# A conditioned feed-forward kernel: the first block's gathered weights by row gathers and register-addressed DMAs in place of a round trip through DRAM

## The reference

```python
w = weights[conditions]                       # (128, 32, 32) from a table of 200 x 32 x 32
h0 = einsum('bct,bcd->bdt', x, w)             # x (128, 32, 256)
logits = h0 @ gate_w                          # gate_w (256, 8), the two largest are summed: scale
h = square(relu(h0 @ up_w))                   # up_w (256, 1024)
y = h @ down_w + scale * (h0 @ expert_weight) # down_w (1024, 256), expert_weight (256, 256)
out = x + (y - mean(y)) * rsqrt(var(y) + eps) * gamma + beta
```

## Time and profile before

| | |
|---|---|
| median of 3 runs | 238.65 us (238.57 to 238.71) |
| the profiled execution: its own time | 238.47 us |
| its span (first to last instruction) | 236.5 us |
| mean granted TensorE clock over the span | 0.985 of full speed |
| PE busy (matmuls) | 225.8 us, 96% of the span |
| DVE, ACT, POOL busy | 147.2, 107.2, 132.3 us |

### The profile page before, as it was taken

How to read it: one execution, slowest core, us unless ns; L and a number is a source line. 1 busy time by engine, 2 the same in 40 slices (tenths; PEclk the granted TensorE clock), 3 DMA queues, 4 the chain that set the end, 5 groups by cost and what they waited for, 6 DMA issues and landing times.

```text
span 236.5 us, 3575 instructions
## 1 busy us (share of the span) xinstructions
PE 225.8 (96%) x1250; PEld 193.3 (82%) x1250; DVE 147.2 (62%) x376; ACT 107.2 (45%) x184; POOL 132.3 (56%) x120
## 2 busy tenths in 40 slices
PE   7489999999999999999999999999999999999991
PEld 3178887888888888888888888888888988888991
DVE  1254696656667666566666666567666566666785
ACT  2247984554455444544444444544443544444200
POOL 4404877465644675365645675455754665566522
PEclk9959999999999999999999999999999999999999
DMA  5679991000110002000020002000020002000021
GB/s 189 199 231 229 204 346 48 4 1 0 48 43 0 1 0 91 1 0 0 13 79 0 3 0 89 1 3 0 1 89 3 0 0 89 4 0 0 35 79 67
DMA packets 15713, 12.95 MB, mean 55 GB/s; under 512 B 5168, under 2 KB 14896, under 8 KB 15696
## 3 DMA queue, kind: packets, MB, share of 16 engines
q1 hardware_dynamic: 15520, 12.14, 17.2%
q0 software_dynamic: 176, 0.59, 0.8%
HBM read 7.94 MB, written 4.78 MB: 54 GB/s over the span
## 4 chain that ended last, share of the span: by engine, by line
PE 86%; DMA 4%; DVE 3%; POOL 2%; issue 2%; ACT 1%; SPq 1%; POOLq 0%; DVEq 0%
PE up_ps L230 35%; PE down_ps L268 24%; PE down_ps L270 12%; PE hid_ps L217 5%; PE moe_ps L286 3%; PE moe_ps L284 3%; PE moe_ps L285 3%; DMA moe<-in_L_cond_weights_dram,cond_col 1%; POOL sq_lo L471 1%; DMA w_first_by_batch<-moe 1%; DVE down_hl L429 1%; DMA cond_col<-in_itok_B_dram 1%; DMA wd<-w_first_by_batch 1%; PE moe_ps L217 1%; POOL x_sb L480 1%
## 5 line engine op out<-in xcount | busy, mean ns | idle before, releaser
L471 POOL TENSOR_TENSOR sq_lo<-square,sq_hi 128x512 fp32r<-128x512 f32 x64 | 83.7, 1308 | 71.1 <-DVE square L369 70.8
L268 PE MATMUL down_ps<-down_hl,sq_hi 128*128 128x512 f32 x248 | 88.8, 393 | 0.3 <-POOL sq_lo L471 0.3
L270 PE MATMUL down_ps<-down_hl,sq_lo 128*128 128x256 f32 x248 | 69.6, 280 | 0.0
L369 DVE SCALAR_TENSOR_TENSOR square<-up_ps,relu 128x512 f32<-128x512 f32 x64 | 44.0, 687 | 38.3 <-ACT relu L323 38.3
L268 PEld LDWEIGHTS down_ps<-down_hl,sq_hi 128*128 128x128 f32 x248 | 46.5, 188 | 11.3 <-issue 0.7
L323 ACT ACTIVATE relu<-up_ps 128x512 f32<-128x512 f32 x64 | 38.2, 597 | 35.0 <-PE up_ps L230 34.7
L230 PE MATMUL up_ps<-hid_hi,up_hi 128*128 128x512 f32 x128 | 52.5, 410 | 0.0
L230 PE MATMUL up_ps<-hid_hi,up_lo 128*128 128x512 f32 x128 | 50.6, 395 | 0.0
L270 PEld LDWEIGHTS down_ps<-down_hl,sq_lo 128*128 128x128 f32 x248 | 46.7, 188 | 2.3
L325 ACT ACTIVATE sq_hi<-relu 128x512 fp32r<-128x512 f32 x64 | 40.5, 633 | 2.0
L230 PE MATMUL up_ps<-hid_lo,up_hi 128*128 128x512 f32 x128 | 40.0, 394 | 0.0
(11 more groups left out here) (44 smaller groups left out, 207.2 us busy)
## 6 DMA issues: line engine op xcount, KB each, us to landing
x_sb<-in_x_dram SPq DMA_DIRECT2D x8, 512.0 KB, 6.4
out_dram<-result SPq DMA_DIRECT2D x7, 512.0 KB, 2.9
result<-in_L_ffn_up_w_dram SPq DMA_DIRECT2D x2, 512.0 KB, 4.6
result<-in_L_ffn_down_w_dram SPq DMA_DIRECT2D x1, 1024.0 KB, 5.7
w_by_batch<-moe SPq DMA_DIRECT2D x1, 512.0 KB, 3.7
out_dram<-result SPq DMA_DIRECT2D x4, 128.0 KB, 1.7
wd<-w_by_batch SPq DMA_DIRECT2D x4, 96.0 KB, 5.9
eg_raw<-L_ffn_expert_weight_dram SPq DMA_DIRECT2D x1, 256.0 KB, 2.5
```

Source lines behind the costliest of these rows:

```text
L268: pe.matmul(dst[:, :], a_hi, down_hl[:, c, :, :].rearrange("p s t -> p (s t)"), start=(c == 0), stop=False)
L270: mm = pe.matmul(dst[:, T:2 * T], a_lo, down_hl[:, c, 0, :], start=False, stop=(c == CH - 1))
L369: dve.scalar_tensor_tensor(square[:, c % 2, :], up_ps[c % UPB][:, :], 0.0, relu[:, c % 2, :], ALU.max, ALU.mult).then_inc(square_done, 1)
L471: pool.tensor_tensor(sq_lo[:, j % 2, c, :], square[:, c % 2, :], sq_hi[:, j % 2, c, :].bitcast(f32), ALU.subtract).then_inc(sq_lo_done, 1)
```

## The change

- SP loads the first 16 conditions into one partition (`cond_row`), and then x of block 0. The full column `cond_col` is loaded later, behind the expert weights and the second half of up_w.
- ACT issues two DMAs at the start: `cond_span` (each partition p gets five conditions from number p // 32 on, so that the condition of its batch row in group 0 and in group 1 stand at two fixed places) and the first half of up_w. It then takes its table load with a small activation on `minus_half`.
- **Groups 0 and 1**: POOL fills `partition` with the partition's number (iota), DVE makes the row numbers `rows = 32 * condition + channel` from it, POOL gathers 128 rows of 128 bytes for each group into `w_pair` (channel to a partition already), and DVE copies four 32x32 pieces of each into `wd`.
- **Groups 2 and 3**: SP (group 2) and ACT (group 3) load four conditions each into registers and issue four DMAs each from the table straight into `wd`.
- `wd` of the later groups is zeroed on POOL behind the two row gathers; the gather of all 128 rows comes after that, and waits for `cond_col`. The write to `all_dram` and the reads of it follow on SP.
- `down_w` goes into the last eight groups of `x_sb`, so it needs no wait and is issued ahead of x of block 1. The x of the last two blocks waits for `down_lo_ready`. The four splits of down move to (0, 5), (0, 6), (0, 7), (1, 0).
- On PE the eight conditioning products of block 0 come in the order in which weights arrive, the first two up chunks are interleaved (`up_rounded`, `up_rest`), `WARM` is 20. On ACT and DVE `hidden(0, k)` stands ahead of the expert split, and `split_up(1)` behind the first chunk.

```diff
-WARM = 26
+WARM = 20
+SPLIT_DOWN_AT = [(0, 5), (0, 6), (0, 7), (1, 0)]
+PAIR = 2
+SPAN = Q * (PAIR - 1) + 1
...
-        down_raw = result_flat.rearrange("p (c t) -> p c t", c=CH)
+        down_raw = x_sb[:, GROUPS - CH:GROUPS, :]
...
+        def conditions(engine, g):
+            _, values = nc.values_load_multi_w_load_instructions(
+                cond_row[0:1, Q * g:Q * g + Q], [engine],
...
+        def weights_of(row):
+            return cond_w[bass.ds(row, 1), :, :].rearrange("s c d -> (s c) d")
...
         def _(sp):
-            sp.dma_start(cond_col[:, :], cond.rearrange("(b o) -> b o", o=1)).then_inc(cond_landed, 16)
+            sp.dma_start(cond_row[:, :], cond.rearrange("(o b) -> o b", o=1)[:, 0:TILES * Q]) \
+                .then_inc(cond_row_landed, 16)
             sp.dma_start(x_sb[:, groups(0), :], x_rows[:, groups(0), :]).then_inc(x_landed[0], 16)
-            sp.dma_start(up_raw[:, :, up_cols(0)], up_rows[:, :, up_cols(0)]).then_inc(up_landed[0], 16)
-
-            sp.wait_ge(first_gathered, 16)
-            sp.dma_start(first_dram, w_first).then_inc(first_written, 16)
-            sp.dma_start(up_raw[:, :, up_cols(1)], up_rows[:, :, up_cols(1)]).then_inc(up_landed[1], 16)
+            sp.wait_ge(cond_row_landed, 16)
+            values = conditions(mybir.EngineType.SP, PAIR)
             sp.wait_ge(wd_zeroed[0], 1)
-            sp.wait_ge(first_written, 16)
             for q in range(Q):
-                sp.dma_start(wd[C * q:C * q + C, groups(0), D * q:D * q + D], first_by_q[q]) \
-                    .then_inc(wd_landed[0], 16)
+                sp.dma_start(wd[C * q:C * q + C, PAIR, D * q:D * q + D], weights_of(values[q])) \
+                    .then_inc(wd_first_landed[PAIR], 16)
+
+            sp.wait_ge(pair_gathered[PAIR - 1], 16)
...
+            def conditioning_first():
+                pe.wait_ge(x_landed[0], 16)
+                pe.wait_ge(spread_done, Q)
+                condition(0, 0, 0)
+                condition(0, 1, 0)
+                pe.wait_ge(wd_first_landed[2], 16 * Q)
+                condition(0, 0, 2)
+                condition(0, 1, 2)
+                pe.wait_ge(wd_first_landed[3], 16 * Q)
+                condition(0, 0, 3)
+                pe.wait_ge(spread_done, 2 * Q)
+                condition(0, 0, 1).then_inc(hid_done, 1)
+                condition(0, 1, 3)
+                condition(0, 1, 1).then_inc(hid_done, 1)
...
+            act.dma_start(cond_span[:, :], bass.AP(tensor=cond.tensor, offset=0, ap=[[1, Q], [0, C], [1, SPAN]])) \
+                .then_inc(cond_pair_landed, 16)
+            act.dma_start(up_raw[:, :, up_cols(0)], up_rows[:, :, up_cols(0)]).then_inc(up_landed[0], 16)
...
+            dve.scalar_tensor_tensor(rows[:, :], cond_span[:, 0:SPAN:Q], float(C), chan[:, :].to_broadcast([P, PAIR]),
+                                     ALU.mult, ALU.add).then_inc(rows_ready, 1)
+            dve.wait_ge(wd_zeroed[0], 1)
+            for g in range(PAIR):
+                dve.wait_ge(pair_gathered[g], 16)
+                for q in range(Q):
+                    part = slice(C * q, C * q + C)
+                    dve.tensor_copy(wd[part, g, D * q:D * q + D], w_pair[part, g, :]).then_inc(spread_done, 1)
...
             pool.memset(minus_half[:, :], -0.5).then_inc(consts_ready, 1)
+            pool.iota(partition[:, :], pattern=[[0, 1]], base=0, channel_multiplier=1).then_inc(partition_ready, 1)
+            pool.wait_ge(rows_ready, 1)
+            for g in range(PAIR):
+                pool.indirect_dma_start(
+                    out=w_pair[:, g, :], out_offset=None, in_=table_rows,
+                    in_offset=bass.IndirectOffsetOnAxis(ap=rows[:, g:g + 1], axis=0)).then_inc(pair_gathered[g], 16)
+            pool.memset(wd[:, TILES:GROUPS, :], 0.0).then_inc(wd_zeroed[1], 1)
             pool.wait_ge(cond_landed, 16)
...
```

More of the change, by code:

```diff
@@ L60, in adaln_ffn @@
         cond_col = sb("cond_col", [P, 1], i32)
+        cond_row = sb("cond_row", [1, TILES * Q], i32)
+        cond_span = sb("cond_span", [P, SPAN], i32)
+        partition = sb("partition", [P, 1], i32)
+        chan = sb("chan", [P, 1], i32)
+        rows = sb("rows", [P, PAIR], i32)
+        w_pair = sb("w_pair", [P, PAIR, D])
+        table_loaded = sb("table_loaded", [P, 1])
         warm = sb("warm", [P, 512], bf16)
@@ L152, in last_tile @@
             return j == BLOCKS - 1 and t == TILES - 1
+        def conditions(engine, g):
+            _, values = nc.values_load_multi_w_load_instructions(
+                cond_row[0:1, Q * g:Q * g + Q], [engine],
+                skip_runtime_bounds_check_because="a condition is an index into the table by the kernel's contract")
+            return values
+        def weights_of(row):
+            return cond_w[bass.ds(row, 1), :, :].rearrange("s c d -> (s c) d")
         block = ctx.enter_context(nc.Block())
@@ L226, in up, with up_rest @@
                 wait(pe, square_done, CH * j + c - UPB + 1)
-                dst, par = up_ps[c % UPB][:, :], j % 2
-                def product(w, k, h, n):
-                    return pe.matmul(dst, w[:, k, P * c:P * c + P], h[:, par, k, :], start=(n == 0),
-                                     stop=(n == 3 * K - 1))
-                product(up_hi, 0, hid_hi, 0)
+                up_product(j, c, up_hi, 0, hid_hi, 0)
                 if j == 0 and c % (CH // UP_PARTS) == 0:
                     pe.wait_ge(up_lo_ready, c // (CH // UP_PARTS) + 1)
-                product(up_lo, 0, hid_hi, 1)
+                up_product(j, c, up_lo, 0, hid_hi, 1)
                 if c == 0:
                     pe.wait_ge(hid_hi_done, K * j + 2)
-                product(up_hi, 1, hid_hi, 2)
-                product(up_lo, 1, hid_hi, 3)
+                up_product(j, c, up_hi, 1, hid_hi, 2)
+                up_product(j, c, up_lo, 1, hid_hi, 3)
+            def up_rest(j, c):
                 if c == 0:
                     pe.wait_ge(hid_lo_done, K * j + 1)
-                product(up_hi, 0, hid_lo, 4)
+                up_product(j, c, up_hi, 0, hid_lo, 4)
                 if c == 0:
                     pe.wait_ge(hid_lo_done, K * j + 2)
-                product(up_hi, 1, hid_lo, 5).then_inc(up_done, 1)
+                up_product(j, c, up_hi, 1, hid_lo, 5).then_inc(up_done, 1)
+            def up(j, c):
+                if j == 0 and c == 0:
+                    up_rounded(j, 0)
+                    up_rounded(j, 1)
+                    up_rest(j, 0)
+                elif j == 0 and c == 1:
+                    up_rest(j, 1)
+                else:
+                    up_rounded(j, c)
+                    up_rest(j, c)
             def down(j, t, half):
@@ L439, in _ @@
                 .then_inc(eg_lo_ready, 1)
-            hidden(0, 0)
-            hidden(0, 1)
             for j in range(BLOCKS + 1):
@@ L460, in _ @@
                             finish(j - 1, c // 2 - 1)
-                    if j == 0 and c >= CH - DOWN_PARTS:
-                        split_down(c - (CH - DOWN_PARTS))
+                    if j == 0 and c == 1:
+                        split_up(1)
+                    if (j, c) in SPLIT_DOWN_AT:
+                        split_down(SPLIT_DOWN_AT.index((j, c)))
             finish(BLOCKS - 1, TILES - 1)
```

82 lines of the change are left out of this document (49 added, 33 removed).

## The result

| | before | changed |
|---|---|---|
| median | 238.61 us (238.10 to 238.71) | 245.56 us (244.89 to 246.40) |
| profiled execution, its span | 238.47, 236.5 us | 244.89, 242.7 us |

The ratio is 1.0297 (95% interval 1.0260 to 1.0334): 3% slower, where I had forecast no change (238.8) and a range that ended at 240.8.

The account below looks back on a forecast made before the run. PE was taken as the bound, so only its idle and half-clock time could be won. Start -1.46, gap -0.31 and clock +1.9 sum to +0.1 us: 238.8 us, no change, own range 238.0 to 239.6, with rivals 235.9 to 240.8.

Parts of the forecast that it names:

- Step 1: Front: cond_span, issued on ACT at about 0.73, lands between 2.75 and 4.05, taken as 3.4.
- Step 2: Front: row numbers at 3.85, gathers at 3.85 and 5.2; groups 0 and 1 land at 6.85 and 8.2.
- Step 3: Front: DVE's eight copies of 32x32 take 0.15 us each; the last four end at 8.9.
- Step 4: Front: groups 2 and 3 through registers land at 6.5 and about 7, hidden behind group 1.
- Step 5: PE: first weights at 7.5 at full clock, conditioning done at 9.7, ready for conditioning(1, 0) at 19.2 instead of 25.46.
- Block 1's chain, 24.0: Block 1's weights, through cond_col, gather, write and reads, let PE start conditioning(1, 0) at 24.0 (22.3 to 26).
- Clock, 1.9: Behind PE's 4.8 us idle before conditioning(1, 0), half clock costs between 0 and 2.6 us, taken as 1.9.
- The 0.31 gap goes, the moved split costs nothing: Block 1: PE's 0.31 us gap for sq_lo goes; the later last down split costs nothing, up to 0.6 without cover.
- From 25.46 the kernel is a fixed length of PE work: From conditioning(1, 0) on: fixed PE work plus a tail, so the change is worth that start's move, idle and clock aside.
- the second, POOL's configuration change: Rival: configuration change ahead of the iota, or other causes, delay second gather past 8.7; slower, 240.4 at 1.5 us; chance 0.21.
- The clock holds, or the chain is shorter: Rival: no clock drop in PE's idle time, 236.9, or block 1's chain 1 us shorter, 235.9; chance 0.29.
- not late: Rival: block 1's weights are not late, conditioning(1, 0) starts 6.3 us earlier, 232.5; chance 0.05.

Follow-up runs that it names:

- h2: Changed kernel with cond_span read by one DMA of outer count 128, eight conditions broadcast to all partitions: 243.72 us, ratio 1.0226.
- e4: Changed kernel with POOL's memset of wd's later groups moved behind the gather of all rows: 245.85 us.
- e5: Changed kernel with POOL's memset of wd's later groups moved right behind the iota: 245.84 us.
- e8: e7 with cond_span loaded by four DMAs of 32 partitions, as in e6: 238.66 us, ratio 1.0040.
- g2: e8 with x of block 1 issued ahead of down_w: 238.03 us, ratio 1.0000.
- g3: g2 with the four down splits back at chunks 4 to 7 of block 0: 237.16 us, ratio 0.9968.
- e1: Kernel before the change plus one unused tile of 480 bytes per partition ahead of warm: 239.61 us, ratio 1.0062.
- e2: Changed kernel with its seven new small tiles allocated last, behind result: 245.26 us.
- e6: Changed kernel with cond_span loaded by four DMAs of 32 partitions instead of one with outer count 4: 245.37 us.
- g1: Changed kernel with down_w and x of block 1 behind the write to DRAM, beta and gamma behind block 1's reads, cond_col left late: 247.47 us, ratio 1.0388.
- e7: Changed kernel with the edits of e3 and g1 together, POOL's memset behind the iota and small tiles allocated last: 238.47 us, ratio 1.0016.
- e3: Changed kernel with the load of cond_col moved ahead of x of block 0 on SP: 243.45 us, ratio 1.0228.

## Why the prediction was wrong

The mechanism was the one that I named: block 1's weights are late next, PE stops at `conditioning(1, 0)`, the clock dips there. The step that failed is the size of block 1's chain: it put the start at 24.0, and it was 28.59. One cost I had not looked for at all. Against the +0.1 of my sum, the start is 4.59 us later, the gap ahead of `down` 0.59 instead of nothing, the clock 0.34 cheaper and the addresses cost 1.05; with 0.18 unplaced that makes 6.1, and the span is 242.7 where the sum gives 236.6.

- **Step 1, `cond_span` at 3.4.** 5.36, above my upper bound of 4.05. I had named the cause, an outer count of four, and priced it by the packet time of a full queue, 0.65 us; h2 puts it at 1.94 (4.62 against 2.68). Worth 1.7 us of the total (h2).
- **Step 2, group 1 landing at 8.2.** SP goes on at 10.04, 1.84 later. The second gather went out at 7.37 instead of 5.2, 2.17 later, nearly all of it `cond_span`; it then took 2.7 us instead of 3.0.
- **Step 3, copies of 0.15.** Right for seven of eight (0.17); the first took 1.52. I read POOL's gathers ahead of the memset, but never asked what the memset, which now ran *with* the copies, does to them. Shown by e4 and e5; worth nothing in total, since block 1 binds.
- **Step 4, register path hidden.** Held: PE waited for DVE's copies, never for the register-addressed DMAs. The two register loads took 0.49 and 0.50 us, less than the 0.6 that I had cited as the least.
- **Step 5, PE ready at 19.2.** 25.98. The first conditioning ends at 15.77 instead of 9.7: 4.0 of this is that the copies end at 12.88 instead of 8.9 (steps 1 to 3), of the other 2.1, 1.7 is the clock at 0.53 over 3.56 us (3.56 x 0.47), which I had at full speed because I expected the weights by 7.5, and the other 0.4 I put down to the held first copy, which left PE nothing to do until then. From 15.77 to 25.98 are 0.7 us more than I had, and two waits show in them, 0.33 for the expert scaling and 0.39 for `up_lo`. It changed little by itself: e5 had PE ready 2.8 us earlier, and it only waited longer.
- **Block 1's chain, 24.0.** Start 28.59, +4.59: `cond_col` issued 1.8 late (steps 1 and 2), 4.4 instead of 2.7 to landing (+1.7), the gather 6.5 instead of 4.3 (+2.2), the write 2.7 instead of 3.7 (-1.0), the reads -0.1. For the gather I had written "up to 1 later since down_w and x move beside it" and then not put it in the sum. **This step decided the sign**; its upper bound of 26 left room for 2 us, and three links slipped by 5.7 together.
- **Clock, 1.9.** 1.56. Right in size, though behind a wait of 2.61 us and not the 4.8 that I argued from; that it came out so near is in part luck.
- **The 0.31 gap goes, the moved split costs nothing.** 0.59 instead of 0.31. e8 and g2, with the last split behind chunk 0 of block 1, show 0.6 and 0.55, g3 with it one chunk earlier has none: this was the 0.6, the bound that I gave for the split without its cover.
- **"From 25.46 the kernel is a fixed length of PE work."** False by 1.05 us: the new tiles change addresses, and PE runs slower on them (e1, e2). No row of before could show it, but the diff did: tiles allocated ahead of others are part of a change.

The rivals: the iota started at 0.86 and took 0.13 us, so the second, POOL's configuration change, had the right sign by a mechanism that did not occur, which is luck; what its last clause held, other causes that move the second gather past 8.7, did. "The clock holds, or the chain is shorter" and "not late" fell.

The part of the change that was to bring a gain can bring a small one: in g3, with the transfers ordered anew, block 1 starts 0.58 us earlier and the clock of the profiled execution stays full, for 0.3%, with an interval that nearly reaches no change.

## What to carry to other kernels

When a change shortens one chain, price the chain that is next with every transfer that now moves beside it, and put a slip of each link in the upper bound together, not one at a time. A transfer's place in the queue has no price of its own: here early conditions won 2.1 us and late bulk lost 1.9, and both together, with the memset out of their way, some 6. Allocate new small tiles behind the large ones, and compare the pace of an undisturbed block first, since it tells an address effect from a wait.

## What the runs showed of the hardware

- **Addresses change the pace of matmuls.** 480 bytes more ahead of `hid_hi` and the tiles behind it moved `up_ps<-hid_hi,up_lo` from 392 to 396 ns in the mean of the later blocks and the first `down` product from 392 to 394, the same in the changed kernel and in e1, and back in e2: 0.15 us in a block of 26.93. 480 is no multiple of 64, so the shift changes the remainder by 32. Whether this remainder is what matters, or another, was not tried.
- **A DVE copy stands still beside a POOL memset.** In h2 the memset stands at the same place in POOL's order and starts 1.42 us earlier than in the changed kernel, as all of the front does:

```profile
6.90 3.10 POOL L581 MEMSET wd<- 128x3584 f32 x1
```

  It ends at 10.00, and the copy from 8.40 ends at 10.03; in the changed kernel 11.42 and 11.45. In e6 the copy began at 8.69, took 2.75 us and ended at 11.44, the memset at 11.41. The copy isn't slowed but held to the memset's end. The Trainium skill (SBUF — State Buffer, Who interferes with whom) says that DVE in its 2-port mode and GpSimd lock a shared pair of ports for the whole instruction, and the other one is blocked. The copy's times agree; that it ran in that mode no row shows.
- **DVE's subtraction of two SBUF tiles is held by POOL's subtraction, not by its memset.** In the kernel before, `up_lo` ran from 7.44 beside a memset until 8.44 and took 1.23 us, as it does alone. Beside one `sq_lo` it took 2.19 and ended 1.07 us behind it (24.49, 23.42); in e4, beside two, it took 3.43 and ended 1.09 behind the second (24.14, 23.05). So the 2.21 in the changed kernel's chain is `up_lo` held to the end of `sq_lo`, because the change moved it behind chunk 0.
- **An indirect gather of 128 rows of 4 KB** takes 4.1 us to landing with nothing beside it (g1), 4.3 in the kernel before and in e7 (253 and 183 GB/s in all, of which some 120 are its own), 6.5 and 8.9 beside 1.5 MB issued around it (314 and 300 GB/s). Four reads of 16 KB take 1.7, and 4 to 5 with down_w and x beside them.
- **Register-addressed DMAs** of 4 KB took 3.6 (g3) to 5.5 us (e3) to landing in the median, where I had taken the 1.98 of the earlier trace rows; nothing waited for them here.
- **The clock stayed full** in g3's profiled execution through idle times of 2.02 and 2.38 us; in the changed kernel one of 4.24 and one of 2.61 were each followed by work at or near half clock (0.53 over 3.56 us, 0.61 over 4.01). The ten executions of g3 have mean clocks of 0.987 to 1.0, so it did not stay full in all of them.
